# A decoder layer on one core: the loop's order of GpSimd's powers and products, ScalarE's first silu and the third norm of the second token block

## What is computed

```python
# part 1: gated linear recurrence
i, f, g = x @ Wi.T, x @ Wf.T, x @ Wg.T
a = sigmoid(f);  b = silu(i) * (1 - a)
h = scan(h_t = a_t * h_(t-1) + b_t)          # over the tokens
y = rmsnorm(h * silu(g)) * w_norm
x = layernorm(x + y @ Wo.T)
# part 2: WKV attention, keys k = x, values v = ctx
y_t = (sum of exp(k_j) v_j decayed by w, the last with bonus u) / (the same sum without v)
x = layernorm(x + y)
# part 3: quantised gated MLP, 512 -> 2 x 1408 -> 512
xq  = quant_dequant(x)                        # 127 levels, one scale per token
h   = silu(xq @ W1q_gate.T) * (xq @ W1q_up.T)
x = layernorm(x + quant_dequant(h) @ W2q.T)
```

## Time and profile before

| | |
|---|---|
| median of 3 runs | 420.44 us (419.89 to 420.63) |
| profiled execution | 419.63 us, span of the core 417.7 us |
| granted TensorE clock, mean | 0.983 of full |
| busy: PE, PEld, DVE, ACT, POOL | 370.7, 290.5, 362.9, 320.9, 232.9 us |
| largest shares of the chain that ended last | PE projections L502 14%, PE MLP L607 6%, POOL Newton product L1269 5% |
| loop, five periods | 132.1 to 350.7 us of the span |

### The profile page before, as it was taken

How to read it: one execution, slowest core, us unless ns; L and a number is a source line. 1 busy time by engine, 2 the same in 40 slices (tenths; PEclk the granted TensorE clock), 3 DMA queues, 4 the chain that set the end, 5 groups by cost and what they waited for, 6 DMA issues and landing times.

```text
span 417.7 us, 7901 instructions
## 1 busy us (share of the span) xinstructions
PE 370.7 (89%) x2756; PEld 290.5 (70%) x2778; DVE 362.9 (87%) x620; ACT 320.9 (77%) x422; POOL 232.9 (56%) x274
## 2 busy tenths in 40 slices
PE   7798899989898899999999999999999998486872
PEld 7797798769775778678866977597759774233331
DVE  3889899869677899989998999899989999998684
ACT  3778599597927899599958996899679976985671
POOL 1574573843526656674667557664767554645451
PEclk9999999999999999999999999999999999888997
DMA  7978356010200020301011020202030202000101
GB/s 246 369 262 322 101 192 240 0 52 27 102 1 2 0 77 1 116 14 50 27 55 73 10 69 25 102 0 75 0 126 0 75 0 75 25 1 2 50 27 51
DMA packets 12842, 31.74 MB, mean 76 GB/s; under 512 B 2038, under 2 KB 5132, under 8 KB 12812
## 3 DMA queue, kind: packets, MB, share of 16 engines
q1 hardware_dynamic: 12812, 31.35, 21.5%
HBM read 27.14 MB, written 4.21 MB: 75 GB/s over the span
## 4 chain that ended last, share of the span: by engine, by line
DVE 26%; PE 24%; ACT 17%; issue 14%; POOL 14%; DMA 2%; SPq 1%; DVEq 0%; POOLq 0%; ACTq 0%
PE proj_ps L502 14%; PE slot_ps L607 6%; POOL den L1269 5%; ACT L1009 3%; DVE hid_top L1648 2%; DVE stats L1584 2%; ACT hqT L974 2%; DVE inp L1487 2%; POOL ring L1294 2%; DVE num L1577 2%; DVE ring L1629 2%; DMA ring<-w_gate_up_dram 2%; DVE x_max L1603 2%; DVE ring L1632 2%; POOL late L1299 2%
## 5 line engine op out<-in xcount | busy, mean ns | idle before, releaser
L1294 POOL TENSOR_TENSOR ring<-ring 128x512 f32<-128x512 f32 (+1 forms) x48 | 62.4, 1302 | 41.2 <-ACT ring L960 41.2
L607 PE MATMUL slot_ps<-w1q,xqT 128*128 128x512 bf16 (+1 forms) x377 | 80.0, 361 | 5.7 <-ACT xqT L951 2.9
L607 PEld LDWEIGHTS slot_ps<-w1q,xqT 128*128 128x128 bf16 x384 | 35.9, 98 | 44.6 <-issue 3.3
L502 PE MATMUL proj_ps<-x_high,proj_high 128*128 128x256 f32 x384 | 64.8, 290 | 0.9 <-ACT proj_high L887 0.5
L502 PE MATMUL proj_ps<-x_low,proj_high 128*128 128x256 f32 x384 | 61.6, 282 | 0.0
L502 PE MATMUL proj_ps<-x_high,proj_low 128*128 128x256 f32 x384 | 61.5, 282 | 0.0
L502 PEld LDWEIGHTS proj_ps<-x_high,proj_high 128*128 128x128 f32 x384 | 53.1, 189 | 2.9 <-issue 0.7
L502 PEld LDWEIGHTS proj_ps<-x_high,proj_low 128*128 128x128 f32 x384 | 52.7, 189 | 0.0
L502 PEld LDWEIGHTS proj_ps<-x_low,proj_high 128*128 128x128 f32 x384 | 52.4, 188 | 0.0
L960 ACT ACTIVATE ring<-ring,zero_bias,x_scale 128x512 f32<-128x512 f32 (+1 forms) x48 | 36.8, 771 | 15.6 <-DVE ring L1629 15.6
L1269 POOL TENSOR_TENSOR den<-den,q_state 128x512 f32<-128x512 f32 x16 | 28.1, 1771 | 35.2 <-ACT q_state L920 35.2
(11 more groups left out here) (146 smaller groups left out, 824.7 us busy)
## 6 DMA issues: line engine op xcount, KB each, us to landing
ring<-w_gate_up_dram SPq DMA_DIRECT2D x11, 512.0 KB, 4.4
forget<-xT_dram SPq DMA_DIRECT2D x8, 512.0 KB, 3.8
x_sb<-x_dram SPq DMA_DIRECT2D x8, 512.0 KB, 3.5
c_sb<-cT_dram SPq DMA_DIRECT2D x8, 512.0 KB, 4.4
out_dram<-late SPq DMA_DIRECT2D x16, 256.0 KB, 2.1
late<-w_down_dram SPq DMA_DIRECT2D x2, 704.0 KB, 6.7
ring<-w_down_dram SPq DMA_DIRECT2D x2, 704.0 KB, 4.4
scale_rows<-scratch_dram SPq DMA_DIRECT2D x2, 704.0 KB, 6.1
```

The costliest lines, as they stand in the source:

```text
L502: last = nc.tensor.matmul(out, a, b, start=(i == 0), stop=(i == len(terms) - 1))
L607: last = nc.tensor.matmul(slot_ps[:, s, half * 512:half * 512 + width], xqT[:, par, d, t * P:(t + 1) * P], w1q[:, d, half * I + at:half * ...
L1294: nc.gpsimd.tensor_tensor(hid, hid, gate_buf[:, at:at + width], ALU.mult).then_inc(hid_ready, 1)
```

## The change

No instruction is added or taken out in the loop's body; the order changes on four engines.

- **VectorE**: `layer_norm_3(n - 1, 1)` goes from between `divide` and `refine` to behind `refine`.
- **ScalarE**: the first `silu(b, par, 0, [0])` goes behind the exponentials and the table load back. `normalise_3` of the second block leaves the end of the iteration and comes in the next one, behind `normalise_1`, as `normalise_3(n - 3, 1)`; the first iteration has none, and the one left over, `normalise_3(9, 1)`, stands behind the loop, behind `normalise_1(7)`.
- **GpSimd**: the two `past_values` and `rstd_3(n - 2, 0)` go ahead of the first product `hidden(b, 0, [0])`; `rstd_3(n - 1, 1)` goes behind `rms_scale`.
- **SyncE**: since the store of the second block now waits for the next iteration's norm, the loads of `xT` and `c` go ahead of it, in the iteration before: `load_xT(b + 3)` and `load_c(b + 2)` behind `load_x(b + 2)`. The first two are issued ahead of the loop, the last iteration has no `load_xT`.

```diff
--- before.py
+++ after.py
@@ -427,11 +427,12 @@
                 sp.wait_ge(y3_ready, n + 1)
                 sp.dma_start(out[b, par], y3[:, par, :]).then_inc(out_stored[par], 16)
 
-            def iteration(b):
-                load_xT(b + 2)
-                load_c(b + 1)
+            def iteration(b, more=True):
                 store(b * TB - 2, b - 1, 0)
                 load_x(b + 2)
+                if more:
+                    load_xT(b + 3)
+                load_c(b + 2)
                 store(b * TB - 1, b - 1, 1)
 
 
@@ -474,11 +475,14 @@
             store_scales(2)
             spread_scales(2)
 
-            with sp.Fori(1, BATCHES - 2) as b:
+            load_xT(3)
+            load_c(2)
+
+            with sp.Fori(1, BATCHES - 3) as b:
                 iteration(b)
-
-
-            load_c(7)
+            iteration(BATCHES - 3, more=False)
+
+
             store(10, 5, 0)
             store(11, 5, 1)
             store(12, 6, 0)
@@ -1016,11 +1020,13 @@
                 n = b * TB
                 split_x(b + 2)
                 normalise_1(b + 1)
-                silu(b, par, 0, [0])
+                if not isinstance(n, int) or n > TB:
+                    normalise_3(n - 3, 1)
                 exp_tables()
                 exponential(b + 1, 0)
                 exponential(b + 1, 1)
                 silu_tables()
+                silu(b, par, 0, [0])
                 read_projection(b + 2, 0)
                 silu(b, par, 0, [1])
                 round_hidden(n - 1, 1, 0)
@@ -1050,7 +1056,6 @@
                 read_hidden(n, 0, 0)
                 read_hidden(n, 0, 1)
                 silu(b, par, 1, [2])
-                normalise_3(n - 1, 1)
                 round_2(b + 1, 1 - par, 0)
                 round_2(b + 1, 1 - par, 1)
                 read_inputs(b + 1, 1 - par)
@@ -1162,6 +1167,7 @@
 
 
             normalise_1(7)
+            normalise_3(9, 1)
             exp_tables()
             exponential(7, 0)
             exponential(7, 1)
@@ -1326,11 +1332,11 @@
                 n = b * TB
                 split_x(b + 2)
                 residual_3(n - 2, 1 - par, 0)
-                hidden(b, 0, [0])
                 past_values(b + 1, 0)
                 past_values(b + 1, 1)
+                rstd_3(n - 2, 0)
+                hidden(b, 0, [0])
                 hidden(b, 0, [1])
-                rstd_3(n - 2, 0)
                 hidden(b, 0, [2])
                 first_token(b + 1)
                 newton(b + 1, 0)
@@ -1340,8 +1346,8 @@
                 pair_squares(b + 2)
                 hidden(b, 1, [1])
                 rstd_2(b + 1)
+                rms_scale(b + 2)
                 rstd_3(n - 1, 1)
-                rms_scale(b + 2)
                 hidden(b, 1, [2])
                 rstd_1(b + 2)
 
@@ -1758,9 +1764,9 @@
                 scale_products(b, 1, [0])
                 divide(b + 1, 0)
                 divide(b + 1, 1)
-                layer_norm_3(n - 1, 1)
                 refine(b + 1, 0)
                 refine(b + 1, 1)
+                layer_norm_3(n - 1, 1)
                 gating(b + 2)
                 scale_products(b, 1, [1])
                 split_states(b + 2)
```

## The result

| | before | after |
|---|---|---|
| median of 12 runs each | 421.12 us (419.89 to 423.44) | 417.42 us (415.5 to 419.49) |
| ratio | 1 | 0.9901, 95% interval 0.9878 to 0.9924 |
| profiled execution, span | 419.63, 417.7 us | 415.5, 413.7 us |
| span ahead of the loop / loop / behind it | 132.1 / 218.6 / 67.0 us | 131.9 / 214.0 / 67.9 us |

The changed kernel is 1.0% faster: 3.70 us between the medians, 4.2 by the ratio. The spread within a kernel, some 4 us, is as large as this difference, so the experiments are compared by the length of the loop in their profiles. Lines of the code shift a little: L502 is now L506, L1608 is L1614, and so on.

A forecast was written before the change was run, and what follows sets the result against it. TensorE was taken to bound the kernel, busy 42.0 of a 43.40 us period. Gains of 0.72 and 3.52, less 0.5 behind the loop, gave 3.74: 420.44 becomes 416.7 us, range 415.4 to 419.3 (8 in 10).

The forecast's parts named there:

- The first gap: TensorE's 0.54 us wait before the output projection: shrinks by 0.41 a period with the norm behind refinement (first period 0.25).
- The second gap: TensorE's 0.47 us wait for rounded inputs: closes, as VectorE's scale falls to 0.17 without GpSimd's product beside it.
- rival 2: GpSimd's power holds VectorE's scale until 259.4, so 0.20 of the gap at the rounding goes: 418.0 us, chance 0.14.
- the sign: Said to show the forecast right: periods of 42.5 to 42.7 us, and 0.4 to 0.7 us more behind the loop.
- The loop: Gain over the five periods: 0.72 us in the first, 0.88 in each of four, together 4.24.
- The last norm: Behind the loop, ScalarE's extra third norm (0.70 us) delays TensorE's down projection: cost 0.3 to 0.7, taken as 0.5.
- The reserve: VectorE's 0.54 us wait for exponentials goes with silu behind them, but GpSimd's products in its scans use it up.
- The loads: SyncE's xT and c ahead of the second store: xT 16 us ahead of need, worth 0, at most 0.1 us.
- 1 (only the first gap): Only the wait before the output projection gives, the scale being held by something else: 419.0 us, chance 0.15.
- 3 (the gating late): GpSimd's products in VectorE's scans keep gating as late as today; only the rounding's gap closes: 418.6 us, chance 0.09.
- 5 (other waits instead): TensorE's gaps are filled by other waits as short, so nothing is gained: 420.4 us, chance 0.06.
- Rival 4: GpSimd's products and powers hold VectorE's scans or numerators for their whole length: slower, near 424.9 us, chance 0.06.

The follow-up runs named there:

- The norm alone: The kernel before with only layer_norm_3(n - 1, 1) moved behind refine on VectorE: loop 216.76 us against 218.64, ratio 0.9922.
- the undone swap: The changed kernel with rstd_3(n - 1, 1) ahead of rms_scale again on GpSimd: loop 216.79 us against 213.97, ratio to before 0.9973.
- The swap alone: The kernel before with only rstd_3(n - 1, 1) moved behind rms_scale on GpSimd: loop 221.99 us against 218.64, ratio 1.0063.

## Why the prediction was right

Forecast 416.7 us and 3.74 us less; measured 417.42 and 3.70 less, 4.13 in the profiled executions. The 0.7 us between 416.7 and 417.42 is the starting point: the longer series put the kernel before at 421.12, not 420.44. Both mechanisms are right; that the total fits better than its terms is luck, as the fourth point shows. Point by point:

- **The first gap**: right to 0.01. The gating was put at 0.41 earlier, tied to ScalarE's gate read. From the period's start TensorE's output projection comes 32.93 us in before (253.43 - 220.50) and 32.52 after (251.07 - 218.55): 0.41. The norm alone gave 1.88 for the forecast's 1.9.
- **The second gap**: the mechanism is right, the term was too small. The scale fell to 0.17 as forecast, and the power beside it held nothing (rival 2 is out). The prediction's reason for taking no hold was thinner than it looked: beside the power of the earlier trace rows VectorE's norm took its usual time, but the power itself took 0.83 us where it takes 0.55 with no norm beside it, and ended 0.04 behind the norm. So the two do meet, and it is the power that was late. I took 0.47 a period, the idle time that the record shows. From the output projection to the turn it is 8.55 us before (261.98 - 253.43) and 7.99 after: 0.56. The down projection's record overlaps the wait by 0.1, as the ends of pipelined matmuls are modelled; the starts tell it better. Five times 0.56 is 2.8, what the undone swap lost (2.82). It also makes the periods 42.3 to 42.5 where 42.5 to 42.7 were named as the sign.
- **The loop**: 4.24 forecast, 4.67 measured; the 0.43 is this term.
- **The last norm**: 0.5 forecast, 0.5 to 0.75 on the chain, and 0.9 behind the loop in the first profile, more than the 0.4 to 0.7 named as the sign; 0.9 is within what that part varies by. I had it as a late down projection. That is the smaller part: the reader is 0.76 later, and 0.54 of it is VectorE's maximum ahead of it, since the scans take 3.47 instead of 2.95. The 0.70 moved GpSimd's products against them (they take 3.85 instead of 3.45). The forecast saw these holds in the loop and not behind it. The two errors, 0.43 too little gain in the loop and some 0.4 too little cost behind it, cancel, so the total is better than its terms. Another 0.23 us fell ahead of the loop, where both kernels do the same work; that part varies by more.
- **The reserve**: right. Holds of 0.8 and 1.0 us were forecast for the scans; they take 4.16 against 2.40 unheld (three steps of 0.58 and a last of 0.66), so 1.8. The size was right because each product's place was put against the scans' one by one.
- **The loads**: 0 by themselves, as said. The swap alone showed what they save when the norm is late: 0.7 us.
- **Rivals**: 1 (only the first gap), 3 (the gating late) and 5 (other waits instead) are each out by the profile: the scale takes 0.17, the gating waits 0.23 for ScalarE's gate read, and TensorE has no new wait in a period. Rival 4's holds are real, 0.5 us a period more than before, and covered.

What the forecast did not say and the experiments show is that the parts depend on each other. The swap of powers is worth 2.8 us once the norm stands in the next period, and costs 3.35 us where the norm is still ahead of the rounding; by the queue's order, moving that norm needs the loads moved. The two gaps themselves add: 1.88 for the norm behind the refinement and 2.82 for the swap against 4.67 together. The reordered first half of the body has no part in the gain.

## What to carry to other kernels

Where a tiny VectorE operation takes several times its usual duration, look at what GpSimd ran beside it and whether the two end together; then put GpSimd's short operations there, and its long products beside VectorE operations that take their usual time with them (the residual that reads PSUM took 1.41 us for its two with the product beside it and without). Measure a gap on a pipelined engine between starts, not by the idle time in its record. And before an operation is moved, list what waits behind it on its own queue and on the transfer queue: the same swap was worth 2.8 us or cost 3.35, by one norm ahead of one rounding.

## What the hardware showed that I had not expected

A GpSimd power of one column (0.55 us) does not hold VectorE's two-column scale (0.17 beside it), while a GpSimd product of 384 columns that began first holds it for what is left of its 1.0 us; begun 0.03 us behind the scale, a product does not. The other way round VectorE's norm of 512 columns does delay that power: 0.82 or 0.83 us beside the norm, in all five periods of the kernel before, and 0.55 or 0.56 with neither the norm nor scans beside it. (Spans on GpSimd are rough, but the start of the operation behind it moves by the same 0.28.) The Trainium skill (SBUF — State Buffer, section SBUF: two separate sides) lets whoever began first keep the shared pair for the whole instruction, where VectorE's operation is in a two-port mode or has two inputs in SBUF (a condition that the prediction left out). The product agrees with this. The power does not: it began first, 0.12 us ahead of the scale and 0.25 ahead of the norm's second half, and held neither. No run shows in which mode these two VectorE operations were. And the half clock behind the loop moved rather than went when TensorE's pauses were partly filled: 6.8 us of it in that profile (windows of 1 us added up, without the stretch at the very end), where the kernel before had 10.2 and the changed one 13.7 and 10.2, but the part behind the loop was no shorter for it.
